# Odd products summed by accumulating transfers, and each quarter's first product moved to GpSimd

## Time and profile before

| | |
|---|---|
| median of three runs | 2505.29 us |
| the profiled execution, its own time | 2503.49 us |
| its span in the profile | 2501.5 us |
| PE / DVE / ACT / POOL busy, share of the span | 94% / 97% / 79% / 88% |
| granted TensorE clock, mean | 0.983 |
| main phase | from about 200 us to about 2474 us |

### The profile page before, as it was taken

The page is one execution under the profiler, slowest core; times in us unless marked ns, Lnnn a source line. Parts: engine busy times, 40 slices in busy tenths (PEclk is TensorE's granted clock), DMA queues, the critical chain, the costliest instruction groups (busy, mean ns, idle before and its releaser), DMA issues. The chain is left out here.

```text
span 2501.5 us, 33084 instructions
## 1 busy us (share of the span) xinstructions
PE 2358.2 (94%) x10524; PEld 1772.9 (71%) x10524; DVE 2420.6 (97%) x2092; ACT 1987.7 (79%) x3496; POOL 2203.1 (88%) x1258
## 2 busy tenths in 40 slices
PE   6737999999999999999999999999999999999996
PEld 3315777777777777777777777777777777777775
DVE  6779999999999999999999999999999999999995
ACT  7736888888888888888888888888888888888783
POOL 4415999999999999999999999999999999999996
PEclk9968999999999999999999999999999999999998
DMA  8962454454545344544544444454445444453433
GB/s 280 310 234 80 131 168 141 115 132 100 150 99 150 91 139 101 133 116 116 137 114 129 110 115 126 113 135 119 134 106 132 108 117 131 100 151 91 108 91 53
DMA packets 150681, 325.34 MB, mean 130 GB/s; under 512 B 16272, under 2 KB 116720, under 8 KB 133872
## 3 DMA queue, kind: packets, MB, share of 16 engines
q1 hardware_dynamic: 78640, 222.33, 26.1%
q0 software_dynamic: 70656, 100.70, 21.6%
q10 hardware_dynamic: 1216, 0.23, 0.0%
HBM read 250.84 MB, written 84.93 MB: 134 GB/s over the span
## 5 line engine op out<-in xcount | busy, mean ns | idle before, releaser
L494 POOL TENSOR_TENSOR ysum<-ysum,prod 128x1024 f32<-128x1024 f32 x480 | 1308.4, 2726 | 33.3 <-DVE prod L920 24.5
L911 DVE TENSOR_TENSOR_SCAN bank_x<-decay,bank_x 128x1024 f32<-128x1024 f32 x512 | 1200.8, 2345 | 0.0
L1117 PE MATMUL bank_l<-ext,w_sb 128*128 128x256 f32 x4096 | 968.9, 382 | 1.0 <-ACT og L689 0.6
L1136 PE MATMUL bank_l<-w_sb,hid 128*128 128x256 f32 x4096 | 957.2, 383 | 0.0
L1136 PEld LDWEIGHTS bank_l<-w_sb,hid 128*128 128x128 f32 x4096 | 762.6, 190 | 163.3 <-issue 67.7
L1117 PEld LDWEIGHTS bank_l<-ext,w_sb 128*128 128x128 f32 x4096 | 755.9, 190 | 135.5 <-issue 23.5
L639 ACT ACTIVATE hid<-bank_l,b_all 128x256 f32<-128x256 f32 x1024 | 430.9, 475 | 338.0 <-PE bank_l L1117 337.6
L920 DVE TENSOR_TENSOR prod<-bank_x,c_all 128x1024 f32<-128x1024 f32 x512 | 650.7, 1271 | 0.1
L854 DVE TENSOR_TENSOR bank_x<-du,bank_b 128x1024 f32<-128x1024 f32 x512 | 646.8, 1263 | 0.0
L630 ACT ACTIVATE decay<-delta,a_sb 128x511 f32<-128x511 f32 x1024 | 640.0, 707 | 1.2
L513 POOL DMA_INDIRECT out<-og,idx_all x256 | 409.3, 1599 | 49.5 <-POOL ysum L494 34.8
(11 more groups left out here) (97 smaller groups left out, 1612.0 us busy)
## 6 DMA issues: line engine op xcount, KB each, us to landing
c_all<-c_rows SPq DMA_DIRECT2D x128, 1024.0 KB, 5.3
w_sb<-in_w SPq DMA_DIRECT2D x32, 1024.0 KB, 7.7
decay<-in_x SPq DMA_DIRECT2D x32, 512.0 KB, 5.2
xn_rows<-decay POOLq DMA_DIRECT2D x32, 512.0 KB, 5.3
out<-yrow POOLq DMA_DIRECT2D x32, 512.0 KB, 7.1
xr<-xn_rows SPq DMA_DIRECT2D x30, 512.0 KB, 6.3
ex<-xn_rows,idx_all POOLq DMA_INDIRECT x256, 2.8
out<-og,idx_all POOLq DMA_INDIRECT x256, 4.9
```

Source lines behind the costliest of these rows:

```text
L494: nc.gpsimd.tensor_tensor(ysum[:, m % 2], first, prod[:, i], ALU.add).then_inc(sum_done, 1)
L911: nc.vector.tensor_tensor_scan(bank_x[:, s % 2], decay[:, k % 2, i].rearrange("p c t -> p (c t)"), bank_x[:, s % 2], 0.0, ALU.mult, ALU.ad ...
L1117: i = nc.tensor.matmul(bank_l[(q + k) % 2][:, (f % 2) * UT:(f % 2 + 1) * UT], w1_sb[:, e2, hc, f * P:(f + 1) * P], ext[:, k % 2, hc], star ...
L1136: i = nc.tensor.matmul(o, hid[:, (k - 1) % 2, f, c * K:(c + 1) * K], w2_sb[:, le2, f], start=False, stop=(f == FC - 1 and c == UB - 1))
```

## The change

In each unit the product of step i = 0 is no longer made by DVE: the scan of that step writes its result to a tile `state` in SBUF, and POOL multiplies it with C (`multiply_c`). The products of i = 0 and i = 2 are added to `ysum` by POOL as before. The products of i = 1 and i = 3 are added to a second sum, `yodd`, by transfers that POOL issues (`link_odd`: SBUF to SBUF, 512 KB, `accum_op=ADD`, each waiting until the one before it has landed); the batch's first odd product is written directly into `yodd` by DVE. Once in a batch POOL adds `yodd` to `ysum` (`join`, in the first unit of the next batch). POOL's work is rewritten as functions, and the order in its unit is new: `take_delta` and `take_du` come first in the last quarter, then the gathers, `multiply_c`, the first add, the first transfer, a scatter, `take_rest`, the second add, the other scatter, `take_lo`, `join`, the output's transfer (now in the second quarter), the second transfer.

```diff
--- before.py
+++ after.py
@@ -115,6 +115,8 @@
         c_all = sb("c_all", [P, 2, STEPS, T])
         prod = sb("prod", [P, 4, HC, T])
         ysum = sb("ysum", [P, 2, HC, T])
+        yodd = sb("yodd", [P, 2, HC, T])
+        state = sb("state", [P, HC, T])
         zabs = sb("zabs", [P, HC, T])
         yrow = sb("yrow", [P, TC, D])
         bc_all = sb("bc_all", [BC, T])
@@ -233,6 +235,9 @@
         bx_done = sem("bx_done")
         scan_done = sem("scan_done")
         prod_done = sem("prod_done")
+        pool_prod_done = sem("pool_prod_done")
+        odd_in = sem("odd_in")
+        joined = sem("joined")
         sum_done = sem("sum_done")
         y_tr = sem("y_tr")
         yrow_done = sem("yrow_done")
@@ -264,6 +269,14 @@
         def batch_of(u, i):
 
             return u // 64 * HALF + u % 8 * UB + i
+
+        def dve_prods(s):
+
+            return s // STEPS * (STEPS - 1) + max(s % STEPS - 1, 0)
+
+        def odd_links(u, i):
+
+            return u // SLOTS * (2 * SLOTS - 1) + u % SLOTS * 2 + i // 2
 
         def expert_of(u):
 
@@ -353,7 +366,8 @@
             def load_c(u):
 
                 held(c_out, (u // SLOTS + 1) * 16)
-                held(prod_done, (u - 1) * STEPS)
+                held(prod_done, dve_prods((u - 1) * STEPS))
+                held(pool_prod_done, u - 1)
                 first = u % SLOTS * STEPS
                 sp.dma_start(c_all[:, u % 2], c_rows[u // SLOTS:u // SLOTS + 1, first:first + STEPS, :]
                              .broadcast_to([P, STEPS, T])).then_inc(c_in[u % 2], 16)
@@ -471,6 +485,64 @@
             gather(1)
             y_before = {}
 
+            def multiply_c(u):
+
+                pool.wait_ge(scan_done, u * STEPS + 1)
+                pool.wait_ge(c_in[u % 2], (u // 2 + 1) * 16)
+                wait(pool, sum_done, u * 2 - 1)
+                nc.gpsimd.tensor_tensor(prod[:, 0], state[:], c_all[:, u % 2, 0][:, None, :].broadcast_to([P, HC, T]),
+                                        ALU.mult).then_inc(pool_prod_done, 1)
+
+            def add_product(u, i):
+
+                b = u // SLOTS
+                if i == 0:
+                    pool.wait_ge(pool_prod_done, u + 1)
+                else:
+                    pool.wait_ge(prod_done, dve_prods(u * STEPS + 3))
+                if u % SLOTS == 0 and i == 0:
+                    pool.wait_ge(skip_done, b + 1)
+                    wait(pool, y_tr, b * 2 - 2)
+                    first = skip[:]
+                else:
+                    pool.wait_ge(sum_done, u * 2 + i // 2)
+                    first = ysum[:, b % 2]
+                nc.gpsimd.tensor_tensor(ysum[:, b % 2], first, prod[:, i], ALU.add).then_inc(sum_done, 1)
+
+            def link_odd(u, i):
+
+                pool.wait_ge(prod_done, dve_prods(u * STEPS + i + 1))
+                wait(pool, odd_in, (odd_links(u, i) - 1) * 16)
+                pool.dma_start(yodd[:, u // SLOTS % 2], prod[:, i], accum_op=ALU.add).then_inc(odd_in, 16)
+
+            def join(b):
+
+                pool.wait_ge(odd_in, (b + 1) * (2 * SLOTS - 1) * 16)
+                pool.wait_ge(sum_done, (b + 1) * SLOTS * 2)
+                nc.gpsimd.tensor_tensor(ysum[:, b % 2], ysum[:, b % 2], yodd[:, b % 2], ALU.add).then_inc(joined, 1)
+
+            def scatter(w, c):
+
+                pool.wait_ge(og_done, w * UB + UB)
+                wait(pool, scattered[w % 2][c], w // 2 * 16)
+                if batch_of(w, c) in y_before:
+                    pool.wait_ge(y_added, 16 * (batch_of(w, c) + 1))
+                pool.indirect_dma_start(
+                    out=out_rows,
+                    out_offset=bass.IndirectOffsetOnAxis(ap=idx_all[:, w * UB + c:w * UB + c + 1], axis=0),
+                    in_=og[:, w % 2, c], in_offset=None, compute_op=ALU.add,
+                ).then_inc(scattered[w % 2][c], 16)
+
+            def add_y(y, units):
+
+                pool.wait_ge(yrow_done, y * 2 + 2)
+                wait(pool, y_added, 16 * y)
+                last = [w for w in range(min(units - 1, NU)) for c in range(UB) if batch_of(w, c) == y]
+                if last:
+                    pool.wait_ge(scattered[last[-1] % 2][y % UB], (last[-1] // 2 + 1) * 16)
+                y_before[y] = True
+                pool.dma_start(out_tiles[y], yrow[:], accum_op=ALU.add).then_inc(y_added, 16)
+
             def main(j):
                 for k in range(BU):
                     m, sl = k // SLOTS, k % SLOTS
@@ -479,51 +551,33 @@
                         pool.wait_ge(resid_out[0], 16 * HALF // UB)
                     if isinstance(j, int) and j == 0 and k == BU - 1:
                         pool.wait_ge(resid_out[1], 16 * HALF // UB)
-                    for i in range(STEPS):
-                        n = sl * STEPS + i
-                        s = b * N + n
-                        if there(b, NB):
-                            pool.wait_ge(prod_done, s + 1)
-                            if n == 0:
-                                pool.wait_ge(skip_done, b + 1)
-                                wait(pool, y_tr, b * 2 - 2)
-                                first = skip[:]
-                            else:
-                                pool.wait_ge(sum_done, s)
-                                first = ysum[:, m % 2]
-                            nc.gpsimd.tensor_tensor(ysum[:, m % 2], first, prod[:, i], ALU.add).then_inc(sum_done, 1)
-                        if sl == 3 and i == 0 and there(b, NB) and there(b + 1, NB):
-                            take_delta(b + 2, (m + 1) % 2)
-                            wait(pool, bx_done, b * N)
-                            take_du(b + 2, (m + 1) % 2, (j * 2 + (m + 1) // 2 + 1) * 16)
-                        if sl == 1 and i == 0 and there(b, NB) and there(b + 1, NB):
-                            take_rest(b + 2)
-                        if sl == 2 and i == 1 and there(b, NB) and there(b + 1, NB):
-                            take_lo(b + 2)
-                        if i == 0:
-                            if there(u + 2, NU):
-                                gather(u + 2)
-                        if i in (1, 2) and there(u - 2, NU):
-
-                            w, c = u - 2, i - 1
-                            pool.wait_ge(og_done, w * UB + UB)
-                            wait(pool, scattered[w % 2][c], w // 2 * 16)
-                            if batch_of(w, c) in y_before:
-                                pool.wait_ge(y_added, 16 * (batch_of(w, c) + 1))
-                            pool.indirect_dma_start(
-                                out=out_rows,
-                                out_offset=bass.IndirectOffsetOnAxis(ap=idx_all[:, w * UB + c:w * UB + c + 1], axis=0),
-                                in_=og[:, w % 2, c], in_offset=None, compute_op=ALU.add,
-                            ).then_inc(scattered[w % 2][c], 16)
-                        if i == 3 and sl == 0 and there(b - 2, NB):
-                            y = b - 2
-                            pool.wait_ge(yrow_done, y * 2 + 2)
-                            wait(pool, y_added, 16 * y)
-                            last = [w for w in range(min(u - 1, NU)) for c in range(UB) if batch_of(w, c) == y]
-                            if last:
-                                pool.wait_ge(scattered[last[-1] % 2][y % UB], (last[-1] // 2 + 1) * 16)
-                            y_before[y] = True
-                            pool.dma_start(out_tiles[y], yrow[:], accum_op=ALU.add).then_inc(y_added, 16)
+                    if sl == 3 and there(b, NB) and there(b + 1, NB):
+                        take_delta(b + 2, (m + 1) % 2)
+                        wait(pool, bx_done, b * N)
+                        take_du(b + 2, (m + 1) % 2, (j * 2 + (m + 1) // 2 + 1) * 16)
+                    if there(u + 2, NU):
+                        gather(u + 2)
+                    if there(u, NU):
+                        multiply_c(u)
+                        add_product(u, 0)
+                        if sl > 0:
+                            link_odd(u, 1)
+                    if there(u - 2, NU):
+                        scatter(u - 2, 0)
+                    if sl == 1 and there(b, NB) and there(b + 1, NB):
+                        take_rest(b + 2)
+                    if there(u, NU):
+                        add_product(u, 2)
+                    if there(u - 2, NU):
+                        scatter(u - 2, 1)
+                    if sl == 2 and there(b, NB) and there(b + 1, NB):
+                        take_lo(b + 2)
+                    if sl == 0 and there(b - 1, NB):
+                        join(b - 1)
+                    if sl == 1 and there(b - 2, NB):
+                        add_y(b - 2, u)
+                    if there(u, NU):
+                        link_odd(u, 3)
 
             through(main, NJ)
 
@@ -696,7 +750,7 @@
                         if pair == 0 and sl == 3 and there(b - 1, NB):
                             take_yrow(0, b * 2 - 1, b * 16 - 16)
```

(29 more changed lines are left out.)

## The result

The changed kernel takes 2600.25 us (median of four, 2589.94 to 2607.21) against 2502.78 before: ratio 1.0386, 95% interval 1.0368 to 1.0403. The profiled execution took 2605.37 us, span 2603.4. Forecast were 2544 us, range 2442 to 2600. The direction was right, the size was not: 97 us measured where 39 were forecast, just outside the range.

A forecast was written before the change was run, and what follows sets the result against it. DVE was taken to set the pace at 71.04 us a batch, with POOL next at 72.15 (71.4 + 0.75). 32 x (72.15 - 71.04) = 35.5, plus 4 at the end, beside the median 2505.3, gave 2544 us, range 2442 to 2600.

The forecast's parts named there:

- What bounds before: Main phase: DVE, PE and POOL near full; DVE sets the pace at 71.04 us a batch, POOL has no room.
- PE's bound: PE's own work a batch, between 67.5 and 70.4 us, taken as 69.0: the least the change could reach.
- DVE's part: DVE's four moved products: 0.9 us saved in each unit, 3.6 a batch, so 71.04 becomes 67.4.
- POOL's part: POOL's own work a batch: 70.90 - 7.2 + 7c, 71.4 us, called the term that decides.
- c: POOL's cost of issuing one link_odd transfer, seven a batch: taken as 1.1 us, upper end 1.37.
- the surcharge: Extra issue cost on POOL of an accumulating over a plain transfer: 0.57 to 0.59 us, supposed fixed whatever the pieces.
- Rival (b): POOL's link issue: fewer pieces save nothing, c = 1.37, about 2605 us; chance 0.13.
- Waits that POOL gets: POOL's waits for links to land, normally none: 0.5 us a batch for the output's transfer, 0.25 for products.
- rival (c): Links chain with other transfers: c_all delays each second link, about 2.3 us a batch, 2618 us; chance 0.09.
- I cost these at nothing: Moved POOL work (take_delta, take_du, take_rest some 7 us later, the output's transfer a quarter later): no time added.
- The end: After the last batch: last odd product must land (5 us) and be joined (2.4); 4 us added.

The follow-up runs named there:

- take_rest early: The changed kernel with take_rest moved to the head of POOL's second quarter, ahead of the gathers and the product with C (also written rest_early); 2595.41 us, ratio 1.0366.
- weights cut: The changed kernel with the loads of the experts' weights cut to 16 columns after the first of each buffer; 2573.69 us, one execution.
- c_all held back, moves first: As c_all held back, but SP issues the moves of B's and C's rows ahead of the held-back load; 2571.41 us, ratio 1.0279.
- c_all held back: The changed kernel with take_rest early and c_all's load held until the second link of the unit that last read its buffer has landed; 2557.42 us, ratio 1.0209.
- c_all cut: The changed kernel with the load of c_all cut to 16 of its 512 columns from the third unit on; 2524.1 us, one execution.
- links cut: The changed kernel with each odd transfer cut to 64 bytes a partition, still 128 pieces; 2516.13 us, one execution.
- the kernel that reaches it: The changed kernel with take_rest early, POOL's product with C only in quarters 0 and 2, and c_all's load held back behind SP's moves; 2469.88 us, ratio 0.9871.

## Why the prediction was wrong

The loss per batch is explained by one sum: POOL's own 71.24 and its waits for landing, in all divided by 32. It meets the measured length to 0.0 to 0.3, and to 0.5 in the changed kernel; no run shows where that rest lies. The 71.24 are themselves taken from a kernel whose links carry next to nothing.

| kernel | landing waits, us a batch | 71.24 + waits | measured |
|---|---|---|---|
| changed | 2.5 | 73.7 | 74.2 |
| take_rest early | 2.3 | 73.5 | 73.8 |
| weights cut | 1.8 | 73.1 | 73.4 |
| c_all held back, moves first | 2.0 | 73.2 | 73.2 |
| c_all held back | 1.5 | 72.7 | 72.7 |
| c_all cut | 0.4 | 71.6 | 71.7 |
| links cut | 0.04 | 71.3 | 71.4 |

Point by point:

- What bounds before: right. Three engines near full, POOL without the room that its 95% shows. PE's bound was put at 69.0 and the kernel that reaches it runs at 69.8; 0.8 too low, without effect on the forecast.
- DVE's part: right. `multiply_b` to the next scan is 1424.36 - 1423.05 = 1.31, forecast 1.35; the scan to SBUF takes 2.28 us and the one to PSUM 2.29.
- POOL's part: right. 71.4 was forecast with c = 1.1, 71.24 measured, 1.08. Its reason was half wrong: the issue itself is about 0.95, so not all of the surcharge is fixed, and the 0.30 of gap behind it, 0.13 more than behind an add, is something that the forecast did not see, though the earlier trace rows show it between the two gathers. Two errors cancelled, which is luck. Rival (b) needed 1.37 us for a link; 128 pieces took 0.95, the output's 512 took 1.37. The Trainium skill (DMA: Bandwidth & Descriptors, "Anatomy of one DMA — SWDGE (gpsimd) path") says that many descriptors can be emitted before their number costs anything; these two figures do not bear it out, as far as transfers with different destinations can tell.
- **Waits that POOL gets: this step failed.** "Normally no wait", and 0.5 a batch for the output's transfer, were forecast; 2.5 were measured. The output's transfer was sized nearly right: 15.3 us were spent on the link queued behind it, 0.5 a batch. What was missing is `c_all`. The forecast took it to be requested with the second link, which has 7.3 us to land and more in the last quarter, and left it to rival (c) with a chance of 0.09, priced at 8 us to land. In fact POOL lags behind DVE in the last quarter, after `delta` and `du`, and in every second batch the request meets the first link, which has about 6 us after its issue; it took 11 us from its start to land, since it did not begin before `c_all` was through. 53.7 of the 79.4 us stand there. Rival (c) named the right culprit and gave 2618; that its 2.3 a batch is so near the measured 2.0 is in part luck, as it had neither the place nor the landing time right. 32 x 2.0 us of unforeseen waits are 64 us; the change came out 97 - 39 = 58 us longer than forecast, and the profiled execution, whose waits these are, is 5 us longer than the median.
- "I cost these at nothing", of the moved `take_rest`: wrong in the trace, small in the sum. Its reader on ACT stands at the end of a unit, but ACT, PE and DVE stand in a row behind it. It shows as 160.9 us of DVE's waits, and is worth 0.4 us a batch or about 5 us of the median (2600.25 to 2595.41, with intervals that overlap), because POOL, held up by links, has DVE wait elsewhere otherwise: 139.4 us at its odd products in `rest_early`.
- The end: 4 us forecast, 6 measured. From the end of the last product to the end of the span it was 2501.5 - 2473.84 = 27.7; it is 2603.4 - 2569.96 = 33.4, 5.8 more. The last product of DVE, the last link, the join and the two transfers of the output:

```profile
2568.73 1.23 DVE L991 TENSOR_TENSOR prod<-bank_x,c_all 128x1024 f32<-128x1024 f32 x1
...
2572.38 1.48 POOL L516 DMA_DIRECT2D yodd<-prod  x1
...
2577.77 2.33 POOL L522 TENSOR_TENSOR ysum<-ysum,yodd 128x1024 f32<-128x1024 f32 x1 [0.16 <-DMA yodd<-prod]
...
2584.67 1.35 POOL L544 DMA_DIRECT2D out<-yrow  x1 [1.00 <-DMA out<-og,idx_all]
2593.69 1.29 POOL L544 DMA_DIRECT2D out<-yrow  x1 [7.67 <-ACT yrow L643]
```

## What to carry to other kernels

An in-order engine that waits for its own transfer pays the landing time at the worst moment, not at the median: look for what else is requested at that moment (here SP's load, released by the last product of a unit), with every engine where it will be after the change and not where it is before, and either separate the two or leave the engine room. A collision that is moved can come back at the next link, as it did here. Work is best moved from a bound engine only as far as the others have room: half of the product's move together with the held-back load gave the gain, neither did alone. And a large wait in the trace need not be the cause; undoing it here only moved the idle time one wait further.

## What was not expected of the hardware

A link issued 0.2 us before a load of `c_all` of 1 MB in 8 KB pieces did not move while that load moved, for four microseconds in which the other queue used the engines about 60% of the time; with the weight's 4 KB pieces it shared them, 69 to 36 in share of time. Cutting `c_all` took 67 of 79 us of waits. The load was requested later but moved first: its packets are there from 1387.5 on, and an undisturbed link's first packet comes 1.55 us after its record's start, which would have been 1387.7. With `take_rest` early, 20 links had the load requested 1 to 2 us after their record's start; their first packet moved at 1.54 (median).

The size of the pieces is not what decides, as the same kernel shows. There `c_all` is requested 2.3 us before the first link of the last quarter. In 15 batches nothing more of SP's is requested just then, and the link's first packet moves at 1.57; in 13 the weight is requested right behind `c_all`, 1.9 us before the link, and the first packet moves at 5.4 (medians). One of these links is issued at 642.20. From 644 to 647 the weight's packets of 4 KB moved, and none of the link's queue:

```profile
q1 hardware_dynamic: 194, 0.77, 87.8%
```

So a weight that was requested well before the link held it up too, and one requested 0.5 us behind it shared. Why was not tried.

The accumulating packets of 4 KB took 0.33 us each (68.8% of 16 engines for 3 us over 101 packets), nearly twice the 0.18 of the weight's plain packets of 4 KB beside them, and less than four times the 0.099 of 1 KB.
